# Flamingo block: the first two weight tiles turned by transfers instead of TensorE

## The reference, cut to what matters

```python
# x (8, 100, 2048), ctx (8, 722, 2048), qweight (2048, 1536) int32: four 6-bit values in three words
def xattn(q, k):
    a = jnp.einsum('bqd,bkd->bqk', q, k)
    return jnp.einsum('bqk,bkd->bqd', jax.nn.softmax(a, axis=-1), k)
def ffn(x, qweight, scale, zero_point, bias):
    w = (unpack6(qweight) - zero_point) * scale          # (2048, 2048)
    return jnp.einsum('bsk,nk->bsn', x, w) + bias
x = x + jnp.tanh(g_xattn[0]) * xattn(layernorm(x), ctx)
x = x + jnp.tanh(g_ffn[0]) * ffn(layernorm(x), qweight, scale, zero_point, bias)
```

## Time and profile before

| | |
|---|---|
| median of 3 runs | 578.82 us (577.61 to 582.05) |
| the profiled execution | 578.77 us, of it 577.0 us from the first to the last instruction |
| TensorE's granted clock | 1.000 over the span |
| busy: TensorE, VectorE, ScalarE, GpSimd | 98%, 62%, 50%, 37% |

### The profile page before, as it was taken

The page is one execution under the profiler, slowest core; times in us unless marked ns, Lnnn a source line. Parts: engine busy times, 40 slices in busy tenths (PEclk is TensorE's granted clock), DMA queues, the critical chain, the costliest instruction groups (busy, mean ns, idle before and its releaser), DMA issues.

```text
span 577.0 us, 8618 instructions
## 1 busy us (share of the span) xinstructions
PE 565.8 (98%) x3390; PEld 407.1 (71%) x3390; DVE 358.7 (62%) x684; ACT 287.5 (50%) x447; POOL 214.7 (37%) x187
## 2 busy tenths in 40 slices
PE   7989999999999999999999999999999999999997
PEld 7879969968968977987986996665554444444445
DVE  5577717826836745755673782966949665655443
ACT  3667567568666676765765757545431220210000
POOL 3046178169249339429619709912000000000000
PEclk9999999999999999999999999999999999999999
DMA  7999749327828727747755675788996994962311
GB/s 237 277 321 240 215 149 305 98 81 239 255 86 274 262 84 265 257 119 220 247 173 177 246 236 229 252 304 279 243 233 208 211 260 134 196 161 71 86 55 42
DMA packets 49203, 115.79 MB, mean 201 GB/s; under 512 B 27960, under 2 KB 28216, under 8 KB 40546
## 3 DMA queue, kind: packets, MB, share of 16 engines
q1 hardware_dynamic: 49052, 114.41, 66.3%
q10 hardware_dynamic: 110, 0.82, 0.5%
HBM read 89.26 MB, written 19.66 MB: 189 GB/s over the span
## 4 chain that ended last, share of the span: by engine, by line
PE 85%; DMA 8%; DVE 5%; issue 1%; ACT 1%; SPq 0%
PE S L1161 19%; PE S L1051 13%; PE T L1005 10%; PE pv L1089 8%; PE S L1089 8%; PE S L1053 7%; PE pv L1161 7%; PE pv L1005 6%; DMA raw<-in_ctx 3%; DMA raw<-late 3%; PE pv L1102 3%; PE S L1102 3%; DVE xres L779 3%; DMA xa<-in_x 1%; DVE qT L897 1%
## 5 line engine op out<-in xcount | busy, mean ns | idle before, releaser
L505 POOL TENSOR_TENSOR vlo<-raw,vhi 128x2048 fp32r<-128x2048 f32 (+1 forms) x38 | 174.3, 4614 | 54.9 <-ACT vhi L571 54.9
L1051 PE MATMUL S<-khi,qT 128*100 128x362 f32 x512 | 141.4, 357 | 0.0
L1053 PE MATMUL S<-klo,qT 128*100 128x362 f32 x256 | 85.1, 332 | 0.3
L907 DVE TENSOR_TENSOR klo<-T,khi 128x361 fp32r<-128x361 f32 x128 | 65.9, 529 | 25.1 <-ACT khi L560 24.4
L907 DVE TENSOR_TENSOR klo<-pv,khi 128x361 fp32r<-128x361 f32 x128 | 65.2, 527 | 22.5 <-ACT khi L560 22.0
L560 ACT ACTIVATE khi<-T 128x361 fp32r<-128x361 f32 x128 | 58.6, 475 | 34.8 <-PE T L1005 34.5
L571 ACT ACTIVATE vhi<-raw 128x2048 fp32r<-128x2048 f32 (+1 forms) x38 | 71.9, 1908 | 6.9 <-PE S L1089 6.9
L560 ACT ACTIVATE khi<-pv 128x361 fp32r<-128x361 f32 x128 | 58.5, 476 | 28.3 <-PE pv L1005 28.3
L1161 PE MATMUL S<-raw 128*128 128x512 f16 x320 | 71.6, 379 | 0.0
L1005 PE MATMUL T<-ident,raw 128*128 128x128 f32 (+1 forms) x416 | 64.2, 268 | 3.8 <-DMA raw<-in_ctx 2.5
L1051 PEld LDWEIGHTS S<-khi,qT 128*100 128x100 f32 x512 | 67.7, 167 | 0.0
(11 more groups left out here) (130 smaller groups left out, 740.5 us busy)
## 6 DMA issues: line engine op xcount, KB each, us to landing
raw<-in_ctx SPq DMA_DIRECT2D x24, 1024.0 KB, 10.3
raw<-in_L_ffn_qweight SPq DMA_DIRECT2D x16, 768.0 KB, 8.2
raw<-in_ctx SPq DMA_DIRECT2D x12, 840.0 KB, 10.6
rows_scratch<-xres SPq DMA_DIRECT2D x8, 800.4 KB
xres<-in_x SPq DMA_DIRECT2D x8, 800.0 KB
x_scratch<-xres SPq DMA_DIRECT2D x8, 800.0 KB
raw<-in_ctx SPq DMA_DIRECT2D x12, 512.0 KB, 12.6
late<-x_scratch SPq DMA_DIRECT2D x24, 256.0 KB, 4.3
```

Source lines behind the costliest of these rows:

```text
L505: pool.tensor_tensor(vlo[0:r, k, :], raw[0:r, b % 2, t, 0:D], vhi[0:r, k, :].bitcast(F32), ALU.subtract).then_inc(s_vlo, 1)
L907: dve.tensor_tensor(klo[:, slot, 0:GW], T[k][:, 0:GW], khi[:, slot, 0:GW].bitcast(F32), ALU.subtract).then_inc(s_free[k], 1)
L1051: pe.matmul(into[0:R, g, 0:MW], qT[:, h, c, :], khi[:, slot, :], start=(c == 0 and h == 0), stop=False)
L1053: last = pe.matmul(into[0:R, g, 0:MW], qT[:, 0, c, :], klo[:, slot, :], start=False, stop=(c == CH - 1))
```

## The change

The first two weight tiles no longer go through TensorE. ScalarE converts them in place, in the unpacking buffer (`wn_at(0)`, `wn_at(1)`): tile 0 after `exps(7)` and ahead of `context_hi(6, 3)`, tile 1 after `probs(7)` and ahead of `ln2_norm(5)`. SyncE issues two transposing transfers into `WT[0]`, after `rows_out(5)` and ahead of `x1_out(6)`, each also after batch 6's tiles 4 and 5 are used. VectorE's `unpack(2)` and `unpack(3)` wait for the landing of these transfers, where they waited for TensorE. TensorE's `weights(0)` and `weights(1)` and ScalarE's copies of them are gone, with four uses of the two banks. `weights(2)` and `weights(3)` stay on TensorE. The counts that other waits compare with are shifted by two tiles.

```diff
         def wn_at(n):
             k = n % 2
+            if n < 2:
+                return unp[k].rearrange("p j g -> p (j g)").bitcast(F16)
...
-        for n in range(2):
-            fill("W", n, 2)
...
+        def converted(n):
+
+            return n + 1 if n < 2 else n - RT + 3
+
+        def turned_at(n):
+
+            return 16 * (n // RT + (n % RT < 2))
...
                 nb, rt = divmod(n, RT)
-                if nb >= 2:
+                if nb == 0:
+                    used(LAST - 1, 4)
+                    used(LAST - 1, 5)
+                elif nb >= 2:
                     sp.wait_ge(s_y, (nb - 1) * MT)
-                sp.wait_ge(s_wn, n - RT + 1)
+                sp.wait_ge(s_wn, converted(n))
                 sp.dma_start_transpose(WT[nb % 2][:, :, rt * P:(rt + 1) * P], wn_at(n)).then_inc(s_wt[rt], 16)
...
             rows_out(LAST - 2)
+            weights_turned(0)
+            weights_turned(1)
             x1_out(LAST - 1)
...
                 exps(i + 1)
+                if i + 1 == LAST:
+                    weights_exact(0)
                 if i + 2 < B:
                     ln1_norm(i + 2)
                 context_hi(i, 3)
...
                     probs(LAST)
+                    weights_exact(1)
                     ln2_norm(i - 1)
                     rows_hi(0, 1)
                 context_hi(i + 1, 1)
             context_hi(LAST, 2)
-            weights(0)
-            weights(1)
             rows_hi(1, 0)
...
-                    if 2 <= n < RT + 2:
+                    if n in (2, 3):
+                        dve.wait_ge(s_wt[n - 2], turned_at(n - 2))
+                    elif n in (RT, RT + 1):
                         bk, u = bank("W", n - 2, 1)
                         dve.wait_ge(s_turned[bk], u + 1)
                     elif n >= RT + 2:
-                        dve.wait_ge(s_wn, n - 2 - RT + 1)
+                        dve.wait_ge(s_wn, converted(n - 2))
...
                         if nb == 0:
+                            pe.wait_ge(s_wt[f], turned_at(f))
                             written("W", nb * RT + RT - 1, f)
...
-            attend(LAST, {0: lambda: weights(0), 1: lambda: weights(1), 2: lambda: normed(1, (0, 1)),
+            attend(LAST, {2: lambda: normed(1, (0, 1)),
                           3: lambda: normed(1, (2, 3)), 4: lambda: weights(2), 5: lambda: weights(3)})
```

More of the change, by code:

```diff
@@ L638, in weights_exact @@
                     act.wait_ge(s_pv, B * NCH)
-                elif n not in (2 * RT, 2 * RT + 1):
-                    act.wait_ge(s_wt[(n - 2) % RT], 16 * ((n - 2) // RT))
+                elif n >= 2 and n not in (2 * RT, 2 * RT + 1):
+                    act.wait_ge(s_wt[(n - 2) % RT], turned_at(n - 2))
                 act.wait_ge(s_u, n + 1)
@@ L1119, in weights @@
             def weights(n):
-                if n == 0:
+                if n == 2:
                     pe.wait_ge(s_id, 2)
@@ L1140, in multiply @@
                         for k in range(RT):
-                            pe.wait_ge(s_wt[k], 16 * nb)
+                            pe.wait_ge(s_wt[k], turned_at(nb * RT + k))
                 if nb == 0:
```

## The result

| | before | changed |
|---|---|---|
| median, 6 runs each | 581.48 us (577.61 to 583.13) | 588.21 us (586.33 to 590.73) |
| ratio, 95% interval | | 1.014 (1.0106 to 1.0175) |
| the profiled execution, its span | 578.77, 577.0 | 590.62, 588.7 |
| TensorE's granted clock, mean | 1.000 | 0.988 |

The forecast was no change, 577.1 to 581.2.

A forecast was written before the change was run, and what follows sets the result against it. TensorE's own work was taken as the bound, 85% of the span. Removing 1.80 us, less idle of 0.5 and 1.1 to 1.2, gave -0.1 us: 578.7, stated as 578.8, range 577.1 to 581.2.

The forecast's parts named there:

- The gate at VectorE's line 811: Ahead of `normed(1, (2, 3))`: TensorE idles 1.1 us until line 811 frees its bank, gaining 0.1 us of 1.80.
- The first sign of the gate: At the weight load of `normed(1, (2, 3))`: its 0.26 us wait was read as VectorE standing just ahead of TensorE.
- ScalarE's conversions: On ScalarE, 1.90 us each: tile 0 costs 0; tile 1 makes `rows_hi(0, 1)` 1.0 us late.
- The landings of the two transfers: In SyncE's queue: the first lands at 370.0, the second at 372.1, both in time for VectorE, cost 0.
- `x1_out(6)`: In SyncE's queue behind the two transfers: issued at 370.4, landed at 379.7, before `ln2_norm(6)` at 380.98, cost 0.
- the part on SyncE's queue: Transfers behind the two added ones: pushed by some us, each wanted over 5 us after it lands, so no cost.
- Behind the gate every due time is as before: After `normed(1, (2, 3))`: due times move with TensorE, so nothing comes back or is lost later.
- Rival 2: SyncE's queue becomes the bound at transfer 1's issue and `x1_out(6)` behind it: 580.8 us, chance 0.2.
- The rule of the Trainium skill against the change: Weight tile transposes: 1309 ns per 128x128 block by transfer against 390 on TensorE, advised where output may go to PSUM.
- The figure of its section The three transpose paths: Transposing transfers: 1309 ns per block, block after block 20.9 us a tile; the forecast used the trace's rows instead.

The follow-up runs named there:

- e7: The changed kernel without its two transposing transfers, the rest of the change kept: 579.28 us, ratio to before 0.9992.
- e2: The kernel before plus two plain copies of 512 KB in 256-byte pieces, at the change's place in SyncE's queue: 586.31 us, ratio 1.0113.
- e13: The kernel before, nothing added, with `x1_out(6)` and `next_xres(7)` issued late, directly ahead of `load_rows(2)`: 587.29 us, ratio 1.0126.
- e3: The changed kernel with `load_rows(4)` moved behind `load_w(6)` in SyncE's queue: 581.2 us, ratio to before 1.0022.
- e6: The changed kernel with its two transfers ahead of `load_rows(1)` and `load_rows(4)` behind `load_w(6)`: 579.27 us, ratio to before 1.0005.
- e14: The kernel before plus one plain copy of 512 KB in 256-byte pieces, at the change's place in SyncE's queue: 585.15 us, ratio 1.0107.

## Why the prediction was wrong

Its steps up to the first product held, most of them to 0.1 us:

- *The gate at VectorE's line 811.* Predicted: TensorE waits 0.4 to 0.5 us for line 779 and about 1.1 for line 811, `normed(1, (2, 3))` starts 0.1 us earlier. Measured: 0.36, 0.98, and the start at 380.05 is 0.16 us earlier than the 374.75 of before once the 5.46 us are taken off. The eight transposes behind the wait then took 1.34 us instead of 1.11, so that the first product came 0.1 us late. Of 1.8 us removed nothing came through; e7 shows the same with no transfer in the kernel.
- *The first sign of the gate.* The 0.26 us of the earlier trace rows say nothing of VectorE. The weight loads ahead of it have the same idle time, put down to no engine:
```profile
373.89 0.17 PEld L1102 LDWEIGHTS S<-raw,pT 105*100 105x100 f32 x1 [0.26 <-issue]
```
The gate was real all the same: it stands on the times of line 811, and the 0.69 us worked out from them.
- *ScalarE's conversions.* `ln2_norm(5)` 1.8 us late, `rows_hi(0, 1)` 0.9 late, as worked out.
- *The landings of the two transfers.* The first was put at 9.1 us, bounds 4.3 to 9.5; it took 10.7, outside the bounds. The second took 4.3 (predicted 5.0). VectorE's wait for the first ended before GpSimd's last remainder did, as predicted, so it cost nothing:
```profile
376.93 1.02 DVE L849 TENSOR_SCALAR raw<-raw 128x512 uint16<-128x512 uint16 x1 [4.03 <-DMA raw<-raw]
...
368.52 9.07 POOL L519 TENSOR_TENSOR vlo<-raw,vhi 128x2048 fp32r<-128x2048 f32 x2 [0.29 <-ACT vhi L585]
```
- *`x1_out(6)`.* Predicted to go out at 370.4, 16.1 ahead of the common event; measured 15.4. It didn't make `ln2_norm(6)` late, also as predicted (386.52, right behind ScalarE's copy).

The step that failed, a delay that the sum put at nothing, is the last sentence of the part on SyncE's queue: "The one megabyte that is added pushes transfers behind it by some us, and each is wanted over 5 us after it lands." I checked each load against the engine that reads it. Two things were left out. First, `rows_out(6)` is wanted by the queue itself: SyncE stops at its landing, so it has no slack, and `load_rows(4)` went out right at that landing in before. Second, the loads behind it form a block of 5.7 MB that ends in tile 4's transfer, and that led without slack to TensorE's wait of 1.19 us at 425.63. I took the sentence "Behind the gate every due time is as before" for granted without following this wait. The rows to see it were there: the chain gives DMA 8% of the span, and I spoke of TensorE's 85% alone; the wait at 425.63 was TensorE's longest in the stretch.

Sizes: landing of `rows_out(6)`, taken as unchanged, 6.7 us; measured 13.1. Tile 4's issue, taken as unchanged, 7.2; measured 12.9. From these 2.8 us more of waiting at the last place and 1.0 us at two earlier ones, and 1.6 us of clock, which the prediction didn't have as a term at all: 5.4 of the 6.2. The other 0.8 us are lost around the two smaller waits, 0.39 at each, as told above.

Rival 2 had the right engine and sign (SyncE's queue becomes the bound), with the wrong place: it looked at `x1_out(6)` against ScalarE's `ln2_norm(6)`, which never waited. Its price of 580.8 would have been too small by far. The rule of the Trainium skill against the change (VectorE: DVE Perf Modes, Rules for kernel authors: TensorE where the output may go to PSUM) agrees with the outcome, since no version with the two transfers is measurably faster than before. The figure of its section The three transpose paths doesn't explain the loss: the 20.9 us for a tile that the prediction estimated from it were not seen (the two took 10.7 and 4.3, the slowest anywhere in the changed kernel 16.3), and e2 and e13 lose as much without any added transposing transfer.

## What to carry to other kernels

When a transfer is added, look in the queue for a wait on the landing of another transfer (here a write that is read back): that transfer has no slack, even if no engine reads what it carries, and all that stands behind the wait moves with it. Follow the last wait of the bounding engine in the stretch, however short, back to its start before calling a later stretch unchanged. Issue independent transfers ahead of such a wait: this makes the kernel bear later additions, as in e3 and e6, even where it gains nothing at first.

## What the runs showed of the hardware that I had not expected

- The issue of a transposing transfer of 512 KB held SyncE for 1.7 to 14.1 us. With the same 5.2 MB issued ahead of it over 14.0 us it was 7.2, over 6.6 us 12.9. Plain copies did too: two in pieces of 256 bytes for 8.33 us together behind 1.8 MB, one alone for 0.71.
- In the stretch ahead of `rows_out(6)` an addition cost more than its bytes at the mean rate: 512 KB, 2 us at 260 GB/s, moved a later landing by 2.8 us as a plain copy and by 5.3 as a transposing one. Two old transfers issued 8.3 and 3.0 us later moved it by 7.8 with nothing added (e13).
- A wait of TensorE of 1.2 us left its clock at the full level, one of 3.9 (changed kernel) was followed by two stretches of 4 us at a mean of 0.69 and 0.88, worth 1.6 us, and one of 2.6 (e14) by two at 0.82 and 0.75.
